# Image weights and first keys and values moved by DMA in later, smaller steps, and a new order of matmuls inside each attention unit

## The reference, cut to what matters

```python
q = proj(Wq, bq) / sqrt(32); k = proj(Wk, bk); v = proj(Wv, bv)     # 16 heads of (4096, 32)
attn = softmax(einsum("bnd,bmd->bnm", q, k), axis=-1)               # (16, 4096, 4096)
fuse = einsum("bnm,bmd->bnd", attn, v)
x = conv1x1(concat([x, fuse]), Wf, bf) * m + x * (1 - m)            # m: mask, resized
# second layer: depthwise 3x3 (edge), gate, 1x1 (fusion), depthwise 3x3 (deform), 1x1 (balance), times x
```

## Time and profile before

| | |
|---|---|
| median of 3 executions | 3969.46 us (3961.45 to 3970.14) |
| the profiled execution, its own time | 3962.3 us |
| its span, first to last instruction | 3960.5 us |
| TensorE busy | 3763.7 us, 95% of the span |
| VectorE, ScalarE, GpSimd busy | 77%, 74%, 75% |
| mean granted TensorE clock | 0.981 of full speed |

### The profile page before, as it was taken

The page is one execution under the profiler, slowest core; times in us unless marked ns, Lnnn a source line. Parts: engine busy times, 40 slices in busy tenths (PEclk is TensorE's granted clock), DMA queues, the critical chain, the costliest instruction groups (busy, mean ns, idle before and its releaser), DMA issues. The chain is left out here.

```text
span 3960.5 us, 66571 instructions
## 1 busy us (share of the span) xinstructions
PE 3763.7 (95%) x19317; PEld 2025.6 (51%) x19317; DVE 3048.2 (77%) x5030; ACT 2923.1 (74%) x5512; POOL 2959.9 (75%) x1359
## 2 busy tenths in 40 slices
PE   7899999999999999999999999999999999959797
PEld 4455555555555555555555555555555555424343
DVE  3478878878878887878878787888777878528989
ACT  1258888888888888888888888888888888812212
POOL 3358889888888888888889898889888988920000
PEclk9999999999999999999999999999999999979898
DMA  6942212221122112211221122212221111121111
GB/s 204 278 132 43 44 22 23 44 44 23 23 44 44 23 23 44 44 23 23 44 31 30 23 33 42 33 21 34 44 32 22 23 23 23 12 80 58 51 56 42
DMA packets 297602, 188.49 MB, mean 48 GB/s; under 512 B 199170, under 2 KB 223924, under 8 KB 297156
## 3 DMA queue, kind: packets, MB, share of 16 engines
q1 hardware_dynamic: 297348, 185.18, 23.9%
HBM read 123.28 MB, written 61.47 MB: 47 GB/s over the span
## 5 line engine op out<-in xcount | busy, mean ns | idle before, releaser
L854 DVE TENSOR_REDUCE block_max<-mx 128x1 f32<-128x512 f32 (+1 forms) x3584 | 2523.7, 760 | 641.5 <-PE mx L623 613.5
L763 ACT ACTIVATE prob<-st 128x512 f32<-128x512 f32 x4096 | 2108.2, 614 | 355.8 <-PE st L612 337.4
L396 POOL TENSOR_TENSOR prob_sum<-prob_sum,prob 128x1024 f32<-128x1024 f32 x768 | 1824.1, 2390 | 26.0 <-POOL prob_sum L396 13.4
L612 PE MATMUL st<-queries,keys 97*128 97x512 f32 x4096 | 1589.6, 408 | 53.6 <-issue 30.6
L623 PE MATMUL mx<-keys,max_queries 96*128 96x512 f32 x4096 | 1579.4, 409 | 7.3 <-ACT tail_exp L748 6.6
L396 POOL TENSOR_TENSOR prob_sum<-prob 128x1024 f32<-128x1024 f32 x384 | 914.5, 2382 | 333.2 <-PE acc L655 329.0
L612 PEld LDWEIGHTS st<-queries,keys 97*128 97x128 f32 x4096 | 772.2, 190 | 528.3 <-issue 304.2
L635 PE MATMUL acc<-prob,values 128*32 128x512 f32 x8192 | 989.0, 601 | 0.0
L623 PEld LDWEIGHTS mx<-keys,max_queries 96*128 96x128 f32 x4096 | 778.1, 190 | 402.2 <-ACT tail_exp L748 169.9
L748 ACT ACTIVATE tail_exp<-mx,negated_max 128x1024 f32<-128x1024 f32 x512 | 575.2, 1123 | 99.1 <-DVE negated_max L858 84.3
L635 PEld LDWEIGHTS acc<-prob,values 128*32 128x32 f32 x8192 | 214.5, 109 | 490.5 <-ACT prob L763 272.8
(11 more groups left out here) (102 smaller groups left out, 1180.4 us busy)
## 6 DMA issues: line engine op xcount, KB each, us to landing
max_queries<-q_scratch SPq DMA_DIRECT2D x384, 64.0 KB
queries<-q_scratch SPq DMA_DIRECT2D x384, 64.0 KB
keys<-k_scratch SPq DMA_DIRECT2D x168, 128.0 KB, 5.6
q_scratch<-keys SPq DMA_DIRECT2D x64, 256.0 KB, 4.7
k_scratch<-keys SPq DMA_DIRECT2D x32, 512.0 KB, 5.0
prob<-in_x SPq DMA_DIRECT2D x16, 512.0 KB, 4.0
v_scratch<-prob SPq DMA_DIRECT2D x16, 512.0 KB, 5.2
queries<-negated_max SPq DMA_DIRECT2D x512, 0.5 KB, 2.0
```

Of the source, the lines that this page charges most:

```text
L396: nc.gpsimd.tensor_tensor(psum[k][:, :, :], a, prob[:, (first + i) % RING, :, :], ALU.add).then_inc(added, 1)
L612: nc.tensor.matmul(st[bank(i, p)][:, :], kk[gp][0:SPLIT + 1, h, s * P:(s + 1) * P], qq[p][:, h, :], start=True, stop=True).then_inc(scores, 1)
L763: nc.scalar.activation(prob[:, s % RING, h, :], st[bank(i, p)][:, :], ACT.Exp).then_inc(exp_done, 1)
L854: nc.vector.tensor_reduce(bmax[p][:, hn, k:k + 1], banks.rearrange("p b n -> p (b n)"), AX.X, ALU.max, negate=True).then_inc(mx_taken, 1)
```

## The change

The DMAs of the image weights leave the start of the projection and are issued after step 11. The keys and values of the first pair, which were eight DMAs in one block after step 8, become three keys DMAs after step 8 (first head), three after step 10 (second head) and two values DMAs after step 13, with a semaphore of their own (`values_loaded`) on which TensorE waits before the first unit. The queries of units 0 and 1 move from step 11 to step 13. In attention the groups become 5, 4, 4, 4, 4 and 3 tiles, and the order of the matmuls, the places of the copies, of the scaling and of the tail exponentials change. The number of matmuls, exponentials, maxima and additions stays.

```diff
-GROUPS = [4, 4, 4, 4, 4, 4]
+GROUPS = [5, 4, 4, 4, 4, 3]
...
-ORDER = ("msmVVVmssmsmmsmsmsmsmsVVsmsmsmsmsmsmsmsmsVVsmsmsmsmsmsmsmsmsVVmsmsmsmsmsm"
...
-SCORES_AHEAD = 23
-BLOCKS_AHEAD = 32
+ORDER = ("mmsmsmsmsmsVVsmsmsmsmsmmssmmsVVsmsmssmmsmsmsmsmsVVsmsmsmsmsmsmsmsmVVssmms"
...
+SCORES_AHEAD = 21
+BLOCKS_AHEAD = 28
...
-NUM_AFTER, DEN_AFTER = 12, 15
-SCALE_AFTER = 12
+NUM_AFTER, DEN_AFTER = 11, 17
+SCALE_AFTER = 17
 TAIL_AHEAD = 0
-TAIL_AFTER = [0, 8, 15, 23, 30, 39, 48, 57]
+TAIL_AFTER = [0, 9, 16, 24, 33, 41, 50, 56]
...
+            def load_keys(g, p, part, cols, h, loaded):
+
+                for r, split in enumerate((0, 1, 0)):
+                    row = (g - p + split) * P + p * 64 + h * HD
+                    sp.dma_start(kk[p][r * HD:(r + 1) * HD, h, bass.ds(part * cols, cols)].bitcast(F32),
+                                 scratch["k"][bass.ds(row, HD), bass.ds(part * cols, cols)]).then_inc(loaded, 16)
+
+            def load_values(g, p, part, vals, h, loaded):
+
+                sp.dma_start(vv[p][:, h, :, :].rearrange("p m d -> p (m d)")[:, bass.ds(part * vals, vals)],
+                             scratch["v"][:, bass.ds(g * 2 + h, 1), bass.ds(part * vals, vals)]
+                             .rearrange("p a k -> p (a k)")).then_inc(loaded, 16)
...
-            for w in IMAGE_WEIGHTS:
-                sp.dma_start(scratch[w][:, :], flat(keep[w])).then_inc(put_away, 16)
             for n in range(STEPS):
...
                     load_q(0, 0, qm, qm_loaded)
-                    load_kv(0, 0, 0, parts=1, first=first_keys)
-                    sp.sem_inc(kv_loaded[0], KV_INC - 16 * 5)
+                    load_keys(0, 0, 0, N, 0, first_keys)
+                if n == PLAIN_CHUNKS - 1:
+                    load_keys(0, 0, 0, N, 1, kv_loaded[0])
+                    sp.sem_inc(kv_loaded[0], KV_INC - 16 * 3)
                 if n == PLAIN_CHUNKS:
+                    load_q(1, 1, qm, qm_loaded)
+                    for w in IMAGE_WEIGHTS:
+                        sp.dma_start(scratch[w][:, :], flat(keep[w])).then_inc(put_away, 16)
+                if n == PLAIN_CHUNKS + 2:
                     load_q(0, 0, qq, q_loaded)
-                    load_q(1, 1, qm, qm_loaded)
                     load_q(1, 1, qq, q_loaded)
+                    for h in range(2):
+                        load_values(0, 0, 0, MT * HD, h, values_loaded)
...
+            pe.wait_ge(values_loaded, 32)
```

More of the change, by code:

```diff
@@ L236 @@
 RING = 16
-ORDER = ("msmVVVmssmsmmsmsmsmsmsVVsmsmsmsmsmsmsmsmsVVsmsmsmsmsmsmsmsmsVVmsmsmsmsmsm"
-         "smsmsVVVsmmssmmsmsmsVsssmmVmsmsmsmsmmssmVVsmsmsmssmmmssmmSSSmsmsmssmmsmsms")
-SCORES_AHEAD = 23
-BLOCKS_AHEAD = 32
+ORDER = ("mmsmsmsmsmsVVsmsmsmsmsmmssmmsVVsmsmssmmsmsmsmsmsVVsmsmsmsmsmsmsmsmVVssmms"
+         "msmsmsmVVVmsmsmsmsmsmsmsmVVsmssmVmsmsmsmsmmsmssmVVssmsmmmssmmSssmmsSSmsmss")
+SCORES_AHEAD = 21
+BLOCKS_AHEAD = 28
 INVERT = 57
-NUM_AFTER, DEN_AFTER = 12, 15
-SCALE_AFTER = 12
+NUM_AFTER, DEN_AFTER = 11, 17
+SCALE_AFTER = 17
 TAIL_AHEAD = 0
-TAIL_AFTER = [0, 8, 15, 23, 30, 39, 48, 57]
+TAIL_AFTER = [0, 9, 16, 24, 33, 41, 50, 56]
 TAIL_FIRST = BLOCKS_AHEAD // MB
@@ L347, in main_phase @@
         first_keys = sem("first_head_keys_loaded")
+        values_loaded = sem("first_values_loaded")
         consts = sem("constants_ready")
@@ L431, in _, with load_kv @@
             sp.sem_inc(part_stored, 16)
-            def load_kv(g, p, part, parts=KV_PARTS, first=None):
-                cols, vals = N // parts, MT * HD // parts
-                for h in range(2):
[L439 to L446, removed]
+            def load_keys(g, p, part, cols, h, loaded):
[7 more added lines that the diff above has]
+                             .rearrange("p a k -> p (a k)")).then_inc(loaded, 16)
+            def load_kv(g, p, part):
+                for h in range(2):
+                    load_keys(g, p, part, N // KV_PARTS, h, kv_loaded[p])
+                    load_values(g, p, part, MT * HD // KV_PARTS, h, kv_loaded[p])
             def load_q(u, p, dst, loaded):
```

## The result

The changed kernel takes **3927.88 us** in the median of four executions (3923.54 to 3937.9), beside 3967.47 (3961.45 to 3970.14) for the kernel before: a ratio of **0.9906, 95% interval 0.9883 to 0.9929**. The profiled execution took 3926.37 us, 35.9 less than the one of before, with a span of 3924.6 and a mean granted clock of 0.985.

The account below looks back on a forecast made before the run. TensorE, 95% busy, was taken as the bound, so gains lay in its waits. Terms -10.4 - 1.6 + 19 - 8 + 3 - 30 = -28 took 3962.3 to 3934 us; half the runs' spread made 3938, range 3908 to 3985.

Parts of the forecast that it names:

- the part put on top for the spread of the runs: Whole kernel: half of the 7 us by which the runs' median exceeds the profiled time, lifting 3934 to 3938 us.
- `x` comes early: Projection, between steps 10 and 11: five DMAs fewer ahead of `x` shorten its 13.22 us wait; -10.4 us, plus -1.6.
- The moved block: Projection, behind steps 10, 11 and 13: the moved loads fit in 6 us of DMA slack per step; 0, up to +5.
- One run more: Attention: ten runs of value or sum products a unit instead of nine cost 0.31 us each; +19 us.
- the copy: Attention, ahead of the sums `S`: TensorE waits about 0.05 us more a unit for ScalarE's numerator copy; +3 us.
- The first score: Attention, next unit's first score: 0.4 us more room cuts the wait for the maxima by 0.13 a unit; -8 us.
- The held time: Attention, behind the last two value products: moving the queries' load removes two thirds of 0.73 us a unit; -30 us.
- a mean unit of 50.0 us: Attention, sign to look for: mean of 62 units 50.0 us instead of 50.48, with the shortest unit at 49.8.
- rival (b): Whole kernel: only the projection wins, with a small part of the stall, say a quarter; 3955 us, chance 0.15.
- Rival (a): Attention: the stall belongs to the place behind the last `V`, not the load, and stays; 3964 to 3968 us, chance 0.20.
- Rival (c): Attention: `S` waits for a copy 0.5 us late, +31 us, 3999 us; chance 0.20, half beyond 3985.
- (d): Projection: wait and keys only change places, step 12 or 13 waits for `x`; costs 10 of 12 us, with any other rival.

Follow-up runs that it names:

- e4: Kernel before with one more SyncE wait, so the next queries, and keys and values behind them, load after the first sum: 3987.43 us, ratio 0.9869.
- e1: Kernel before with only the change's SyncE projection queue and the wait on `values_loaded`; order, groups and places as before: 4027.38 us, ratio 0.9967.
- f3: Kernel before with the six transfers of the next queries left out from the third unit on: 3987.26 us, ratio 0.9962 to before.
- e3: Changed kernel with GpSimd's scaling put back behind the 13th addition (SCALE_AFTER 12): 3994.7 us, ratio 0.9884 to the kernel before.
- g3: Kernel before with only the store of the last unit's result put behind the sums: 4027.46 us, ratio 1.0006.
- g1: Kernel before with store, next queries, and next pair's keys and values all behind the sums by one SyncE wait: 3981.9 us, ratio 0.9875.
- e2: Kernel before with only GpSimd's scaling moved behind all 18 additions (SCALE_AFTER 17): 3989.87 us, ratio 0.9873.
- f1: Kernel before with the new order, groups and places (scaling late too), SyncE's old projection kept: 3966.28 us, ratio 0.9917.
- f2: Kernel before with the change's SyncE projection part and the scaling behind all 18 additions, old order and groups: 3954.61 us, ratio 0.9881.
- g2: Changed kernel with one SyncE wait putting store, queries, keys and values behind the sums: 3962.24 us, ratio 0.9830 to the kernel before.

## Why the prediction was right

Its time, 3938, is 10 us over the measured median, of which the part put on top for the spread of the runs is 3.5. Term by term, against the profiled execution:

- **`x` comes early, -10.4 and -1.6.** Together -12.0, measured -11.1 at the first sums. The wait is 3.39 where the terms left 2.8. One step failed: "with less than 3 us of wait I expect no fall of the clock". There were 3.39 us, and it fell.
- **The moved block, 0.** Right: no new wait in steps 12 to 15; the slack of the earlier trace rows is now used (0.98 instead of 0.77).
- **One run more, +19, and the copy, +3.** The shortest unit grew from 49.48 to 49.71, so +0.23 x 62 = +14 for both. The fixed part per run was taken too dear. The last of the 62 units is left out here; it is shorter in both kernels, 49.28 and 48.55.
- **The first score, -8.** Measured against the shortest of the same kernel, the mean share of that place went from 0.24 to 0.12: -0.12 x 62 = -7.
- **The held time, -30.** 0.77 to 0.26: -0.51 x 62 = -32. These three sum to -25, beside -27.9 measured; the short last unit is 1 of the rest, and some 2 us went at other places of the units. That the -30 came out so well is luck: two thirds was a weighing of all (45 us) against nothing, and that a third of the held time would stay was not foreseen.
- **Not foreseen, +3.1:** the last unit has no units behind it to fill its order, and its sums wait 7.01 us for the copy.

So the terms gave -16 for the units, where -27.9 was measured, and the half spread put on top took the forecast further up. Two numbers of the prediction don't follow from its own terms: a mean unit of 50.0 us is what the whole 0.73 us would give, the sum as taken gives 50.2 (measured 50.03); and rival (b), a quarter of the stall, comes to 3957, or 3960 with the half on top, not 3955.

Rival (a), that the stall belongs to its place and not to the load, is refuted for the part that went away, by e4; the 0.7 to 1.0 us that stay there on the slower chips are what it had claimed. Rival (c), that `S` waits for the copy, is refuted by the shortest unit, (d) by e1. The rule in the Trainium skill, page "SBUF — State Buffer", section "Who interferes with whom", by which a DMA never contends with a compute engine, would have SyncE's timing be indifferent. e4 changes nothing but that timing, and wins 1.3% (interval 1.1 to 1.6%), so here the measurement decides. What the runs can't say is at which shared thing the two meet, and so not whether it is one of those that the page speaks of.

The reason given was right in part. Moving the queries, and the keys and values behind them, out from under the last products does give the gain (e4: GpSimd untouched). But "the load of the next queries" was too narrow: never loading them (f3) gives less than half of it, and keys in their place seem to do the same harm (argued from f3's two kinds of units, not shown by a run of its own). And the new order with the scaling in its old place takes a third of the held time by itself (e3 against e1), which I had not priced: I had put the whole term on the place. **Open:** what holds the results for up to 5.6 us (g3), and why 0.7 to 1.0 us a unit stays on the slower chips when store, queries, keys and values are all out of the way.

## What to carry to other kernels

Where several engines resume late at once and no engine is at work, look at what SyncE has in flight at that place, and try its transfers at another place: here one wait, which put them behind the sums, did as much as a whole new order with the late scaling. Test an order and a place separately: here one moved pair of instructions (the scaling) and a moved block of DMAs gave as much in the old order as in the new one. And count runs of one kind of product: one more, with the copy that it waits for, was 0.23 us a unit, 14 us in all.

## What the runs showed of the hardware

- **Transfers under GpSimd's additions crawl.** In f3, DMA is 0.74 busy at 26 GB/s in 1276.00 to 1277.50, where GpSimd adds all the time, and 1.05 busy at 378 GB/s in 1281.50 to 1282.50, when GpSimd is idle; in g1 it is 0.39 busy at 14 GB/s beside an addition. A load issued there is in flight far longer than its size says. The keys of the next pair say the same: between 400 and 3400 us, one of their DMAs of 128 KB takes 8.5 us from issue to landing in the median of f3 and 5.6 in the kernel before, and 2.4 to 2.5 in the changed kernel, e4 and g1, which issue them when GpSimd is mostly done. No run changed GpSimd's work alone.
- **A hold costs twice.** After the longest, TensorE's clock falls to the lower level: in g1 it is 0.50 in 1127 to 1129 and 16 sums take 2.87 us instead of 1.92. Between 330 and 3480 us the granted clock is low for 99 us in e1 and 41 in e2; half of the difference, up to 29 us, is by this estimate what the clock costs of the 55 us by which e1 is the longer of the two behind its first sums (spans 4028.6 and 3984.8, first sums at 304.5 and 315.6).
- **The same units are held, on every chip.** Unit by unit, over 61 units, the held time of the kernel before correlates with itself on the fourth chip by 0.74, with the changed kernel by 0.66, with e1, e2, f1 and f2 by 0.66 to 0.76. As soon as SyncE's part in attention is another (e4, f3, g1 to g3) it is 0.01 to 0.16; g1, g2 and g3 agree with each other by 0.60 to 0.72. So the hold isn't chance, and it isn't in TensorE's own order (e3 and e1 differ in it and agree by 0.78): it goes with what SyncE does. The order of the DMAs alone can't be it, since e4 and g1 issue the same DMAs in the same order as the kernel before and only wait once more; nor is any shift in time enough, since e2 issues its queries later and keeps the pattern. What in SyncE's part sets it is open. How long the holds last differs by chip: 0.77 and 1.57 us a unit for one kernel on chips 1 and 4, which is 0.80 x 62 = 50 of the 66 us between their two profiled executions.
